# An AdaLN block in fp32 on one core: the value products of a head in one burst instead of two, four side slots instead of three, and the high halves of rows and keys written by ScalarE

## The reference

```
h = layernorm(x) * (1 + ca) + sa
q = h @ q_w.T + q_b          # 16 heads of 32
k = h @ k_w.T + k_b;  v = h @ v_w.T + v_b     # one head each
attn = softmax(where(causal, -inf, q k^T / sqrt(32)))
x = x + ga * ((attn @ v) @ o_w.T + o_b)
h = layernorm(x) * (1 + cb) + sb
x = x + gb * ffn(h)          # Hadamard transforms, SiLU gate, width 2048
```

## Time and profile before

| | us |
|---|---|
| median of 3 runs | 1978.73 (1975.44 to 1981.24) |
| profiled execution | 1982.4 |
| its span | 1980.6 |
| PE busy | 1902.7 (96%) |
| DVE busy | 1392.6 (70%) |
| ACT busy | 833.0 (42%) |
| POOL busy | 462.1 (23%) |
| mean granted TensorE clock | 0.984 |

### The profile page before, as it was taken

One profiled execution on the slowest core, in us unless ns is written; L12 is line 12 of the kernel. 1 busy time (PEld: TensorE's weight loads), 2 busy tenths in 40 slices (PEclk: granted clock), 3 DMA queues, 4 the chain that ended last, 5 costly groups with the idle time before them and its releaser, 6 DMA issues.

```text
span 1980.6 us, 39650 instructions
## 1 busy us (share of the span) xinstructions
PE 1902.7 (96%) x15040; PEld 1582.5 (80%) x15040; DVE 1392.6 (70%) x3247; ACT 833.0 (42%) x1551; POOL 462.1 (23%) x525
## 2 busy tenths in 40 slices
PE   6999999999999999999999999999999999999998
PEld 3677777777777667667888789999999999999997
DVE  6788787777668666684467797777676777767755
ACT  3366455555555554473222442333333323333221
POOL 2244455445444444362010010010000100101000
PEclk8899999999999999999999999999999999999999
DMA  7432243333332455635347989778788797887884
GB/s 228 131 97 67 77 122 102 94 82 96 107 109 60 130 167 172 221 123 177 138 138 281 359 312 347 286 288 333 287 314 323 294 345 287 291 329 290 330 306 165
DMA packets 118709, 416.19 MB, mean 210 GB/s; under 512 B 26349, under 2 KB 39917, under 8 KB 104313
## 3 DMA queue, kind: packets, MB, share of 16 engines
q1 hardware_dynamic: 106856, 363.27, 53.7%
q10 hardware_dynamic: 11664, 50.40, 6.7%
HBM read 318.16 MB, written 61.10 MB: 191 GB/s over the span
## 4 chain that ended last, share of the span: by engine, by line
PE 46%; DVE 5%; ACT 2%; DMA 1%; issue 1%; SPq 0%; POOL 0%; DVEq 0%; ACTq 0%
PE banks L1810 22%; PE banks L1900 15%; PE banks L1680 8%; PE banks L1776 1%; DVE ln_stats L1254 1%; PE banks L1770 1%; DMA upgate_items_dram<-items_ring 1%; DVE x_normed L1266 0%; DVE y L1379 0%; DMA upgate_raw<-in_w_ug 0%; ACT silu_gate L911 0%; ACT y_split L896 0%; ACT L911 0%; ACT L917 0%; DVE out_sb L1451 0%
## 5 line engine op out<-in xcount | busy, mean ns | idle before, releaser
L1900 PE MATMUL banks<-d_ring,y_split 128*128 128x512 f32 x1536 | 377.6, 393 | 1.9 <-DVE y_split L1399 1.9
L1007 ACT ACTIVATE probs<-banks 128x512 f32<-128x512 f32 x576 | 314.8, 600 | 149.6 <-PE banks L1946 145.7
L1900 PEld LDWEIGHTS banks<-d_ring,y_split 128*128 128x128 f32 x1536 | 281.9, 188 | 56.6 <-DVE y_split L1399 2.1
L1810 PE MATMUL banks<-h_t_split,items_ring 128*128 128x256 f32 x2280 | 321.2, 284 | 1.9 <-DVE both L1356 1.9
L1810 PEld LDWEIGHTS banks<-h_t_split,items_ring 128*128 128x128 f32 x2280 | 299.0, 191 | 13.7 <-ACT h_t L822 4.0
L1734 PE MATMUL banks<-k_stack,q_stacks 96*128 96x512 f32 (+3 forms) x768 | 255.5, 376 | 26.7 <-DVE max_all L1166 12.4
L1946 PE MATMUL banks<-q_stacks,k_stack 98*128 98x512 f32 (+3 forms) x768 | 254.2, 373 | 4.5 <-DMA q_stacks<-neg_max_rows 3.9
L1810 PE MATMUL banks<-input_sums,items_ring 128*128 128x256 f32 x1710 | 236.2, 283 | 0.0
L1108 POOL TENSOR_TENSOR probs<-probs 128x1024 f32<-128x1024 f32 x64 | 153.4, 2396 | 334.0 <-ACT probs L1007 334.0
L1978 PE MATMUL banks<-probs,values 128*32 128x128 f32 (+1 forms) x3328 | 222.8, 322 | 3.1 <-POOL probs L1128 3.1
L1810 PEld LDWEIGHTS banks<-input_sums,items_ring 128*128 128x128 f32 x1710 | 218.9, 192 | 0.0
(11 more groups left out here) (180 smaller groups left out, 2715.1 us busy)
## 6 DMA issues: line engine op xcount, KB each, us to landing
items_ring<-upgate_items_dram SPq DMA_DIRECT2D x94, 1792.0 KB, 7.3
d_ring<-down_split_dram SPq DMA_DIRECT2D x128, 512.0 KB, 8.1
q_stacks<-q_split SPq DMA_DIRECT2D x192, 128.0 KB, 2.9
upgate_raw<-in_w_ug SPq DMA_DIRECT2D x32, 512.0 KB, 4.8
upgate_items_dram<-items_ring ACTq DMA_DIRECT2D x8, 1792.0 KB, 7.5
upgate_items_dram<-items_made ACTq DMA_DIRECT2D x8, 1792.0 KB, 6.7
x<-in_x SPq DMA_DIRECT2D x32, 256.0 KB, 3.0
o_group<-o_and_sums SPq DMA_DIRECT2D x256, 32.0 KB
```

The lines of the kernel that those rows point to most:

```text
L1007: nc.scalar.activation(pr[:, probs_slot(H, u), :], score_bank[:, at % SLOTS_SCORE, :], ACT.Exp, scale=SCALE).then_inc(exped, 1)
L1810: last = nc.tensor.matmul(item_bank(g, item), weights[:, a, item, k * P:(k + 1) * P], by_key(item_input(blk, item, m))[:, k, :], start=(k ...
L1900: last = nc.tensor.matmul(acc[:, t, :], ys[s][:, a, t * P:(t + 1) * P], dr[g % D_RING][:, m, :], start=(f == 0 and a + m == 0), stop=(f == ...
```

## The change

The two parts of a head's value products become one burst. It stands behind unit 5 (`WEIGH_UNIT`) of the next head, directly behind maximum 5, the transposed maxima (moved from unit 2) and, where there is one, a fold. The list is cut anew: 14 products in part 0 and 27 in part 1 instead of 21 and 24, with the same 60 blocks. The output has one bank (7) instead of two, so part 0 also waits for the copy of the head before. The bank that comes free is the fourth side slot. ScalarE copies the output behind unit 5, and the transposed maxima behind its exponential of unit 2, which is as early as PE's order allows. Folds that stood behind unit 4 go behind unit 5. `modulate` and `keys_values` read the PSUM bank twice on ScalarE and write the high half as well as the fp32 copy; DVE's casts go. The semaphores of the fold loads are merged.

```
+WEIGH_UNIT, SCORES_AHEAD = 5, 3
...
-    if 0 < H < heads - 1:
-        units[TOP_UNIT].append(("top", H + 1))
     if 0 < H < heads - AHEAD:
         for i in range(NS):
             units[i].append(("max", H + AHEAD, i))
+    if 0 < H < heads - 1:
+        units[WEIGH_UNIT].append(("top", H + 1))
...
-FOLDS = [("across", left, u) for left, us in ((18, (4, 8)), ...
+FOLDS = [("across", left, u) for left, us in ((18, (5, 8)), ...
...
-    SLOTS_SCORE, SLOTS_SIDE = 3, 3
-    score_bank, side, obank = banks[:, 0:3, :], banks[:, 3:6, :], banks[:, 6:8, :]
+    SLOTS_SCORE, SLOTS_SIDE = SCORES_AHEAD, 4
+    score_bank, side, obank = banks[:, 0:3, :], banks[:, 3:7, :], banks[:, 7, :]
...
             def modulate(key):
-                nc.scalar.activation(kv[:, i % 2 * HALF:(i % 2 + 1) * HALF], side[:, r, :], ACT.Identity,
-                                     bias=mod[:, 0, k, b:b + 1], scale=mod[:, 1, k, b:b + 1]).then_inc(side_free[r], 1)
+                for out in (ht[:, 0, k, h * HALF:(h + 1) * HALF], kv[:, i % 2 * HALF:(i % 2 + 1) * HALF]):
+                    last = nc.scalar.activation(out, side[:, r, :], ACT.Identity, bias=mod[:, 0, k, b:b + 1], scale=mod[:, 1, k, b:b + 1])
+                last.then_inc(side_free[r], 1)
             def keys_values(key):
+                nc.scalar.activation(kst[0:96, key[1] % 2, at], side[0:96, r, :], ACT.Identity, bias=kvb[0:96])
...
             def step(H):                                    # ScalarE
                     side_step(ends[u])
-                    if u == PART_ENDS[0] and H:
+                    if u == WEIGH_UNIT and H:
                         evacuate(H - 1)
-                    side_step(units[u])
+                    side_step([key for key in units[u] if key[0] != "top" or H == 0])
+                    if u == WEIGH_UNIT - SCORES_AHEAD and H:
+                        side_step([key for key in units[WEIGH_UNIT] if key[0] == "top"])
...
             def split_rows(key):                            # VectorE
-                chain.link(nc.vector.tensor_copy(ht[:, 0, k, at], kv[:, i % 2 * HALF:(i % 2 + 1) * HALF]))
             def stack_keys(b, h):
-                chain.link(nc.vector.tensor_copy(kst[0:96, b % 2, at], kv[0:96, at]))
...
             def weigh(H, part):                             # TensorE
-                    if H >= 2:
-                        pe.wait_ge(o_copied, H - 1)
+                    if H:
+                        pe.wait_ge(o_copied, H)
...
-                    if u == PART_ENDS[0] and H:
-                        weigh(H - 1, 1)
-                    if u == (PART_ENDS[1] if H else FIRST_WEIGHED):
-                        weigh(H, 0)
-            weigh(ALL - 1, 1)
+                    if u == WEIGH_UNIT and H:
+                        for part in range(PARTS_OF_HEAD):
+                            weigh(H - 1, part)
+            for part in range(PARTS_OF_HEAD):
+                weigh(ALL - 1, part)
```

More of the change, by code:

```diff
@@ L52 @@
 WEIGHED = [
[L53 to L60 removed]
+    [(0, 0, (0, 4)), (1, 0, (1, 5)), (2, 0, (2, 6)), (3, 0, (3, 7)), (0, "sum", ((0, 3), (6, 7))), (1, "sum", ((6, 6),)),
+     (2, 1, (2, 6)), (3, 1, (3, 7)), (1, 1, (1, 5)), (0, 1, (4,)), (2, 2, (2, 6)), (3, 2, (3, 7)), (0, 2, (4,)), (1, 2, (5,))],
+    [(0, 3, (4,)), (1, 3, (5,)), (2, 6, (6,)), (3, 3, (3, 7)), (0, 4, (4,)), (1, "sum", ((0, 2),)), (2, 3, (6,)),
+     (0, "sum", ((1, 3), (4, 7))), (1, 4, (5,)), (2, 4, (6,)), (3, 6, (7,)), (1, "sum", ((1, 2), (4, 6))), (2, "sum", ((0, 1), (4, 5))),
+     (3, 4, (7,)), (0, "sum", ((3, 3), (5, 7))), (3, "sum", ((0, 0), (4, 4))), (1, 5, (5,)), (2, 5, (6,)), (0, "sum", ((2, 3), (7, 7))),
+     (1, "sum", ((2, 2), (5, 6))), (2, "sum", ((1, 1), (5, 5))), (3, 5, (7,)), (3, 7, (7,)), (0, "sum", (("all", 7),)),
+     (1, "sum", (("all", 6),)), (2, "sum", (("all", 5),)), (3, "sum", (("all", 4),))],
 ]
@@ L92 @@
 PART_ROWS = 32
-PART_BANKS = (6, 7)
+PART_BANKS = (2, 7)
 BESIDE_MAXIMA = {("max", 0, 2 * k + 1): k for k in range(KT)}
@@ L100 @@
 PROJECTION_STEPS = (1, 5)
-FOLDS = [("across", left, u) for left, us in ((18, (4, 8)), (17, (4, 8)), (16, (4, 8)), (15, (2, 4, 6, 8)), (14, (4, 8)), (13, (4, 8)), (12, (4, 8))) for u in us]
-FOLDS += [("along", left, u) for left, us in ((10, (4, 8)), (9, (4, 8)), (8, (4, 8)), (7, (2, 4, 6, 8)), (6, (4, 8)), (5, (4, 8)), (4, (4, 8))) for u in us]
+FOLDS = [("across", left, u) for left, us in ((18, (5, 8)), (17, (5, 8)), (16, (5, 8)), (15, (2, 4, 6, 8)), (14, (5, 8)), (13, (5, 8)), (12, (5, 8))) for u in us]
+FOLDS += [("along", left, u) for left, us in ((10, (5, 8)), (9, (5, 8)), (8, (5, 8)), (7, (2, 4, 6, 8)), (6, (5, 8)), (5, (5, 8)), (4, (5, 8))) for u in us]
 FOLD_RING = 4
@@ L421, in phase @@
     small_in, had_ready = sem("ffn_small_in"), sem("had_ready")
-    across_in, raw_in, again_in = sem("across_in"), [sem(f"raw_in{n}") for n in range(FOLD_RING)], [sem(f"again_in{n}") for n in range(FOLD_RING)]
+    across_in, fold_in = sem("across_in"), [sem(f"fold_in{n}") for n in range(FOLD_RING)]
     fold_hi, fold_out = sem("fold_hi"), [sem(f"fold_out{n}") for n in range(2)]
@@ L754, in keys_values @@
                 r = side_filled(act, key)
-                nc.scalar.activation(kv[:, h * HALF:(h + 1) * HALF], side[:, r, :], ACT.Identity, bias=kvb[:]).then_inc(side_free[r], 1)
+                at = slice(h * HALF, (h + 1) * HALF)
+                nc.scalar.activation(kst[0:96, key[1] % 2, at], side[0:96, r, :], ACT.Identity, bias=kvb[0:96])
+                nc.scalar.activation(kv[:, at], side[:, r, :], ACT.Identity, bias=kvb[:]).then_inc(side_free[r], 1)
             def values(key):
@@ L981, in evacuate @@
                     act.wait_ge(gathered[H % 2], 80 * (H // 2))
-                nc.scalar.activation(oraw[:, H % 2, :], obank[:, H % 2, :], ACT.Copy).then_inc(o_copied, 1)
+                nc.scalar.activation(oraw[:, H % 2, :], obank, ACT.Copy).then_inc(o_copied, 1)
             def round_group(G, half):
@@ L1757, in fold_tile @@
                     pe.wait_ge(across_in, 16)
-                    pe.wait_ge(raw_in[i % FOLD_RING], 16 * (i // FOLD_RING + 1))
+                    pe.wait_ge(fold_in[i % FOLD_RING], 16 * (i // FOLD_RING + 1))
                     r = side_slot(key)
@@ L1761, in fold_tile @@
                 else:
-                    pe.wait_ge(again_in[i % FOLD_RING], 16 * (i // FOLD_RING + 1))
+                    pe.wait_ge(fold_in[i % FOLD_RING], 16 * ((FT + i) // FOLD_RING + 1))
                     r = side_slot(key)
@@ L1892, in down @@
                     if g == 0:
-                        for r in (1, 2):
+                        for r in range(1, SLOTS_SIDE):
                             side_drained(pe, r)
@@ L1976, in weigh @@
                     moving = pr_blocks(places[0], places[-1] - places[0], len(places))
-                    out = obank[row * HD:(row + 1) * HD, H % 2, first * P:(first + len(places)) * P]
+                    out = obank[row * HD:(row + 1) * HD, first * P:(first + len(places)) * P]
                     last = nc.tensor.matmul(out.rearrange("p (a n) -> p a n", n=P), weights, moving, start=row not in begun, stop=part == 1 and last_of[row] == i)
```

13 lines of the change are left out of this document (2 added, 11 removed).

## The result

The changed kernel takes 2035.01 us (median of four runs, 2031.36 to 2038.89), the kernel before 1977.63 beside it: ratio 1.028, 95% interval 1.026 to 1.031. I had forecast 1988, slower, with 2010 as the upper end. The direction was right, and the size was short by a factor of six: +57 where I had +9.5.

The account below looks back on a forecast made before the run. Two regimes: heads limited by PE, and heads where PE and DVE nearly tie. Terms without the clock summed to +3.5 us, the clock added 6; +9.5 on the profiled 1982.4 gave 1992, as median 1988; range 1956 to 2010.

Parts of the forecast that it names:

- Step 1: Value products of a head: one burst takes 3.4 us, 0.13 less than two; PE gains 0.35 to 0.4 a dense head.
- Step 2: Plain and statistics heads: DVE idles about 2.2 us, heads become 9.2 and 9.8 us; +7 us (+2 to +9).
- Step 3: Nine rows heads: DVE's subtraction waits for ScalarE's row activations; 12.0 us against 10.83, +11 us (+4 to +15).
- Step 4: Heads around projections: dense PE and four slots give 13.6 us against 14.48; -14 us (-8 to -18).
- Step 5: Remaining heads and prologue: keys and values -3 us, queries +1, folds +1, prologue +1.5 with 1 given back.
- Step 6: TensorE's clock: about five more falls, as PE waits before bursts in plain and rows heads; +6 us (0 to +18).
- Rival (c): Clock falls in every head where PE now waits for DVE: 24 heads, 36 us, 2018 us in all; chance 0.07.

Follow-up runs that it names:

- the first filler: Changed kernel with the products of the maxima computed twice in 24 chosen heads, output unchanged; 2040.92 us, ratio 1.032.

## Why the prediction was wrong, step by step

- **Step 1 (one burst) held for the burst.** 82 records, 3.39 us. Projection heads of the first batches took 13.70 to 13.99 for 13.6. But the 0.35 to 0.4 that PE was to gain in a dense head is there in one of three only, at 0.30: these heads take 13.70, 13.99 and 13.99 in the changed kernel and 14.00 each with two bursts.
- **Step 2 (DVE and the burst) had the right mechanism, too small.** Top waits for maximum 2, 6.11 after the burst's end for 5.8: the negation ended at 3.7, behind GpSimd's sum, as I had it, and the first later maximum starts 0.35 behind it; with 0.2 from top to the burst a plain head is 9.70 for 9.2, one with statistics 10.07 for 9.8. The 15 heads of these kinds cost 19 us (15.2 + 4.0) for 7, some 4 of them by the clock. (My own head times, 9.2 and 9.8 over these 15 heads, add up to 11, not to 7.)
- **Step 3 (rows) was near its upper bound.** At full clock these heads would be about 12.6 (14.0 on the mean, less 1.4, an estimate), for 12.0: +16 for +11. Both holds that I named were there: DVE waits 5.22 us for ScalarE's activation in head 26, and GpSimd's second sum holds it there, if on the second negation (1.23 us) and not on the subtraction. The other 13 us are the clock's, by the same estimate.
- **Step 4 (projections) came near its sum, in part by luck.** The five heads around the projections of each batch (20-24, 36-40, 52-56) gave -2.3, -2.4 and -7.2, -11.9 for -14; I had -4.7 in each. The queries elsewhere (4, 8, 16, 32, 48) gave -4.8 for +1. And the fourth slot gives most of it, not the burst or the copies: with two bursts the sum of all these heads is the same, with the copies alone the projection heads gain nothing.
- **Step 5 left out the last six heads** of the last batch (turns and Hadamard products beside the rest). They cost 19.3 us, of which 9 to 12 are the clock's (23.9 us more at the lower level). This is a term missing from the sum. What the rest of it is I haven't traced; with two bursts these heads take 69.4. Keys and the next heads gave +4.9 for -3, with 10.2 us more at half clock, folds +1.3 for +1.
- **Step 6 (the clock) is the one that failed most.** I had five more falls, +6, at most +18. The heads show 72.2 us more at half clock, 21 stretches of 3.4; at 1.3 to 1.7 each, 28 to 36 of the 55.6 us that the heads lost, by estimate; at the lowest price seen, 1.0, it would be 21. Rival (c) had 36 us for 24 falls, and I gave it 0.07; even its 2018 falls short. Of the stretches nine are in rows heads, seven in the last six, three beside keys, three in statistics heads and none in plain ones (the queries have one less). For rival (c) the trace of before had rows 10; against it I set the mean clock of 0.98, an average over heads in which PE waited less (0.9 us in a rows head, and none of those nine fell). By the rule of the Trainium skill that stood beside rival (c) ("TensorE: Matmul & The Clock Gate", "A second HAM failure mode: psum-queue depth-cycling") the clock goes back and forth when PE idles in pieces between groups; the changed trace agrees (0.50 behind 2.79 busy of 4.38 us), and so does the first filler, which takes idle pieces away, in six of nine rows heads.
- **What I didn't ask** was which part pays. The fourth slot by itself, with two bursts kept, gives 38 us, the copies 10. I had counted their gain only where one burst left it over.

The heads without the clock's part then sum to +20 to +28 for +3.5, an error nearly as large as the clock's: 15 plain and statistics, 16 rows, -17 projections and queries, 1 folds, some 9 in the last six. So the mechanism of steps 2 and 3 was right and its sizes too small, one class of heads was forgotten, and the number of the clock's falls was read from the wrong average.

## What to carry to other kernels

When two engines are coupled by a ring, compare the longest absence of the producer with what the consumer can take from full slots: 1.9 us of work against 3.4 of burst here, and 1.87 was the longest before. Merging two such absences saved 0.14 us and opened a hole of 2.4 (1.26 in plain head 31 with two bursts). Where a change puts a wait for another engine in front of PE in many heads, price the clock per head and not by the mean of the kernel before. And take a change of several parts apart: two of the three parts here are worth 44 us (the fourth slot with the single output bank, and the copies), and the kernel with two bursts, one output bank, four slots and ScalarE's copies (1934, 2.2% faster than before) beats both.

## What the runs showed of the hardware

- A stretch at half clock of 3.4 us cost a head of this kernel 1.0 to 1.7 us. More PE work, placed in the waits ahead of the burst, took 6.8 us off the nine rows heads that had it; that kernel was 11 us faster in all.
- VectorE's small operations on SBUF were held by a GpSimd sum of SBUF tensors until it ended: 8 columns in 0.17 to 0.21 us free, 0.37, 0.87, 1.14 and 1.23 beside one. Maxima that read PSUM ran on beside it: two over 256 columns of head 31 took 0.48 and 0.42 during its sum.
- A plain maximum over 256 columns took 0.41 us and one over 512 0.68; in a row, 0.33 and 0.60 from start to start.
